# A mixture-of-experts stage on Trainium2: second products entered before the last activations, and an output finished in two parts

## What is computed

```python
probs = softmax(xt @ Wr + br)
top_p, top_idx = jax.lax.top_k(probs, 2)
weights = top_p / top_p.sum(-1)
xn = (xt - mu) * rsqrt(var + 1e-5)
xe = xn[None] * ln_g[:, None] + ln_b[:, None]
h = gelu(einsum('end,edh->enh', xe, W1) + b1)
y = einsum('enh,ehd->end', h, W2) + b2
out = x + sum over the node's two experts of weight * y
```

## Time and profile before

| what | us |
|---|---|
| median of 3 runs | 2840.2 |
| the profiled execution, its own time | 2840.06 |
| span of the profiled execution | 2838.0 |
| share of the span with PE busy | 83% |

### The profile page before, as it was taken

The page is one execution under the profiler, slowest core; times in us unless marked ns, Lnnn a source line. Parts: engine busy times, 40 slices in busy tenths (PEclk is TensorE's granted clock), DMA queues, the critical chain, the costliest instruction groups (busy, mean ns, idle before and its releaser), DMA issues.

```text
span 2838.0 us, 39531 instructions
## 1 busy us (share of the span) xinstructions
PE 2366.4 (83%) x14254; PEld 1777.4 (63%) x14254; DVE 1033.1 (36%) x2750; ACT 450.3 (16%) x1227; POOL 884.5 (31%) x661
## 2 busy tenths in 40 slices
PE   5185552577859999999997889999999995999997
PEld 2151110354547777777775457888888894888886
DVE  7688885233321111112115854112211455111111
ACT  0030000000015100003203742001111003222222
POOL 6888888887840000000003320000000001333332
PEclk6595555798979999999999999999999996999999
DMA  9922223886460899992144000444344434667665
GB/s 337 317 1 0 0 1 48 237 225 182 69 181 15 176 221 258 227 209 82 58 151 146 1 1 12 148 143 138 127 139 151 160 121 139 204 191 228 189 206 169
DMA packets 298688, 397.91 MB, mean 140 GB/s; under 512 B 178182, under 2 KB 242125, under 8 KB 298507
## 3 DMA queue, kind: packets, MB, share of 16 engines
q1 hardware_dynamic: 115530, 268.24, 29.7%
q10 hardware_dynamic: 110560, 108.20, 15.5%
q0 software_dynamic: 72496, 20.10, 8.4%
HBM read 279.36 MB, written 99.82 MB: 134 GB/s over the span
## 4 chain that ended last, share of the span: by engine, by line
PE 63%; POOL 20%; issue 7%; DVE 5%; DMA 3%; ACT 1%; DVEq 0%; SPq 0%; ACTq 0%; POOLq 0%
PE ps L2085 14%; POOL odd_counts L622 10%; POOL at_counts L622 10%; PE ps L2414 9%; PE ps L2416 9%; PE ps L2510 7%; PE ps L2501 7%; PE ps L2011 5%; PE ps L2103 3%; PE ps L2216 2%; PE ps L2370 2%; PE ps L2347 2%; DMA odd_counts<-harena 1%; PE ps L2262 1%; PE ps L2483 1%
## 5 line engine op out<-in xcount | busy, mean ns | idle before, releaser
L2414 PE MATMUL ps<-harena,ring 128*128 128x257 f16 (+1 forms) x2500 | 540.3, 272 | 5.2 <-DVE harena L1728 3.9
L2416 PE MATMUL ps<-harena,ring 128*128 128x256 f16 x2400 | 534.4, 271 | 0.0
L2085 PE MATMUL ps<-ring,harena 128*128 128x320 f16 (+1 forms) x3740 | 506.9, 298 | 1.4 <-ACT tarena L830 0.8
L2085 PEld LDWEIGHTS ps<-ring,harena 128*128 128x128 f16 x3740 | 367.1, 98 | 138.0 <-issue 3.1
L622 POOL DMA_INDIRECT at_counts<-harena x208 | 327.3, 1574 | 81.7 <-issue 79.0
L622 POOL DMA_INDIRECT odd_counts<-harena x208 | 328.9, 1581 | 67.1 <-issue 62.5
L1250 DVE SCALAR_TENSOR_TENSOR late<-ps,ring 128x512 f16<-128x512 f32 x416 | 287.4, 746 | 20.8 <-PE ps L1973 9.7
L1973 PE MATMUL ps<-harena,ident 104*128 104x512 f32 x208 | 186.1, 1011 | 116.7 <-DVE late L1250 115.7
L2414 PEld LDWEIGHTS ps<-harena,ring 128*128 128x128 f16 x2500 | 243.1, 97 | 40.3 <-DVE harena L1728 6.1
L2416 PEld LDWEIGHTS ps<-harena,ring 128*128 128x128 f16 x2400 | 232.2, 97 | 29.9
L700 POOL IOTA harena<- 1x32 int32 x1 | 0.2, 184 | 685.5 <-DVE xrows L1810 685.5
(11 more groups left out here) (418 smaller groups left out, 2459.1 us busy)
## 6 DMA issues: line engine op xcount, KB each, us to landing
ring<-at_counts SPq DMA_DIRECT2D x145, 800.0 KB
ring<-L_ffn_W SPq DMA_DIRECT2D x64, 1024.0 KB, 5.3
ring<-ad_counts SPq DMA_DIRECT2D x50, 800.0 KB
at_counts<-tarena ACTq DMA_DIRECT2D x5, 4000.0 KB, 21.5
odd_counts<-tarena ACTq DMA_DIRECT2D x5, 4000.0 KB
ad_counts<-xrows ACTq DMA_DIRECT2D x25, 800.0 KB, 7.7
xrows<-odd_counts SPq DMA_DIRECT2D x20, 800.0 KB
at_counts<-ring ACTq DMA_DIRECT2D x20, 800.0 KB
```

Of the source, the lines that this page charges most:

```text
L2085: ins = M(ps[:, 2 * f + h, 0:c], part[:, t, (2 * k + f) * P:(2 * k + f + 1) * P], chunk[q][:, s, h * HB:h * HB + c], start=(t == 0 and par ...
L2414: ins = M(ps[:, i, 0:wide], lhs, hh[:, t, 0:wide], start=(t == 0), stop=(t == T - 1))
L2416: ins = M(ps[:, i, 0:F], lhs, hl[:, t, :], start=False, stop=False)
```

## The change

There are four edits.

The diff:

```diff
--- before.py
+++ after.py
@@ -273,6 +273,8 @@
         xn = runs(tarena[:, T * F:2 * T * F], a=T)
         hot_lane = runs(tarena[:, 0:2 * T * P], a=2 * T)
         hot_column = harena[:, 0:2 * T * 2 * SC].rearrange("p (j v c) -> p j v c", j=2 * T, v=2)
+        final_row, same_row = hot_lane[:, 0, :], hot_lane[:, 1:1 + CT, :]
+        in_both = late[:, 2490:2490 + CT]
         w1e = [ring[:, s * 4096:s * 4096 + 2048].rearrange("p (d h) -> p d h", d=2) for s in range(2)]
         w2e = [ring[:, s * 4096 + 2048:(s + 1) * 4096].rearrange("p (k o) -> p k o", k=EK) for s in range(2)]
         hT = [harena[:, s * 2048:(s + 1) * 2048].rearrange("p (k n) -> p k n", k=EK) for s in range(2)]
@@ -573,11 +575,12 @@
                     sp.nop(nofuse=True)
                     load_second(e, s)
 
-            sp.wait_ge(y_used, CHUNKS + 2)
-            for b in range(0, NB, 2):
+            sp.wait_ge(y_used, CHUNKS)
+            for b in range(NB):
                 r = slice(b * BC, min((b + 1) * BC, N))
                 sp.dma_start(out[r, :], x_sum[r, :]).then_inc(out_stored, 16)
             sp.wait_ge(out_stored, 16 * NB)
+            sp.wait_ge(y_added, 16 * SC)
 
 
         @block.gpsimd
@@ -746,7 +749,7 @@
             gather_rows(2)
             pool.wait_ge(moe_stored, 16 * 5)
             pool.wait_ge(r_dve, 4)
-            for c in range(CHUNKS):
+            for c in range(CHUNKS - 2):
                 pool.wait_ge(e_y, c + 3)
                 for i in range(UNITS_OF[c]):
                     j = UNIT_AT[c] + i
@@ -757,6 +760,20 @@
                     gather_rows(c + 3)
                 pool.wait_ge(y_added, 16 * sum(UNITS_OF[:c + 1]))
                 pool.sem_inc(y_used, 1)
+
+            for c in (CHUNKS - 2, CHUNKS - 1):
+                pool.wait_ge(e_tps, c + 1)
+                for i in range(UNITS_OF[c]):
+                    j = UNIT_AT[c] + i
+                    nc.gpsimd.indirect_dma_start(out=xin[c % 2][:, i, :], out_offset=None, in_=x_sum,
+                                                 in_offset=bass.IndirectOffsetOnAxis(ap=from_row[:, j:j + 1], axis=0)).then_inc(row_in[c % 2], 16)
+            pool.wait_ge(out_stored, 16 * NB)
+            for c, rows, done in ((CHUNKS - 2, xin[0], CHUNKS + 2), (CHUNKS - 1, yrow[1], CHUNKS + 3)):
+                pool.wait_ge(e_y, done)
+                for i in range(UNITS_OF[c]):
+                    j = UNIT_AT[c] + i
+                    nc.gpsimd.indirect_dma_start(out=out, out_offset=bass.IndirectOffsetOnAxis(ap=to_row[:, j:j + 1], axis=0),
+                                                 in_=rows[:, i, :], in_offset=None, bounds_check=N - 1, oob_is_err=False).then_inc(y_added, 16)
 
 
         @block.scalar
@@ -1086,10 +1103,6 @@
                     for k in range(EK):
                         wait(e_hps, g * (TURN * EK) + (j * EK + k + 1))
                         nc.scalar.activation(hT[s][:, k, 0:n], ps[:, k % 4, 0:n], ACT.Gelu, bias=evc[s][:, k:k + 1]).then_inc(e_gelu, 1)
-            wait(y_used, CHUNKS + 2)
-            for b in range(1, NB, 2):
-                r = slice(b * BC, min((b + 1) * BC, N))
-                act.dma_start(out[r, :], x_sum[r, :]).then_inc(out_stored, 16)
 
 
         @block.vector
@@ -1916,6 +1929,14 @@
             step(V.tensor_tensor(slot_pad, slot_pad, trash_row[:, :], ALU.mult))
             step(V.tensor_tensor(slot_pad, slot_pad, slot_node, ALU.add))
             V.tensor_scalar(to_row, slot_pad, -1.0, None, ALU.add).then_inc(r_dve, 1)
+            V.tensor_scalar(final_row, ident[:, :], slot_pad[:, SC - 1:SC], None, ALU.mult).then_inc(r_dve, 1)
+            dve.wait_ge(r_pe, 4)
+            last_pair = slice(UNIT_AT[CHUNKS - 2], UNIT_AT[CHUNKS - 2] + CT)
+            o.mark(V.tensor_tensor(same_row, ps[:, 7, 0:P].unsqueeze(1).to_broadcast([P, CT, P]), slot_pad[:, last_pair].unsqueeze(2).to_broadcast([P, CT, P]), ALU.is_equal))
+            o.settle()
+            step(V.tensor_reduce(in_both, same_row, AX.X, ALU.max))
+            step(V.scalar_tensor_tensor(out=in_both, in0=in_both, scalar=float(2 * T * P), in1=slot_pad[:, last_pair], op0=ALU.mult, op1=ALU.add))
+            o.mark(V.tensor_scalar(to_row[:, last_pair], in_both, -1.0, None, ALU.add))
 
             def expert_rows(c, uses, s, n):
 
@@ -1933,13 +1954,34 @@
                 step(V.tensor_tensor(rows, ps[:, 4 + s, 0:k * F].rearrange("p (i c) -> p i c", i=k), b2e[s].unsqueeze(1).to_broadcast([P, k, F]), ALU.add))
                 V.tensor_tensor(rows, rows, slot_gate[:, bass.ds(unit, k)].unsqueeze(2).to_broadcast([P, k, F]), ALU.mult).then_inc(e_y, 1)
 
+            def pair_finished():
+
+                dve.wait_ge(row_in[0], 16 * (sum(UNITS_OF[0::2]) + CT))
+                dve.wait_ge(e_y, CHUNKS + 1)
+                V.tensor_tensor(xin[0], xin[0], yrow[0], ALU.add).then_inc(e_y, 1)
+
+            def single_finished():
+
+                gate = slot_gate[:, SC - 1:SC]
+                dve.wait_ge(row_in[1], 16 * (sum(UNITS_OF[1::2]) + 1))
+                dve.wait_ge(w2e_in[1], 32 * (CHUNKS // 2))
+                dve.wait_ge(e_yps, CHUNKS + 2)
+                step(V.tensor_tensor(xin[1][:, 0, :], xin[1][:, 0, :], ps[:, 6, 0:F], ALU.add))
+                step(V.scalar_tensor_tensor(out=xin[1][:, 0, :], in0=b2e[1], scalar=gate, in1=xin[1][:, 0, :], op0=ALU.mult, op1=ALU.add))
+                dve.wait_ge(e_yps, CHUNKS + 3)
+                dve.wait_ge(y_used, CHUNKS)
+                V.scalar_tensor_tensor(out=yrow[1][:, 0, :], in0=ps[:, 5, 0:F], scalar=gate, in1=xin[1][:, 0, :], op0=ALU.mult, op1=ALU.add).then_inc(e_y, 1)
+
             def turn_of_chunks(g, last):
 
                 for j in range(TURN):
                     c, s = g * TURN + j, j % 2
-                    if not (last and j == TURN - 1):
+                    if last and j == TURN - 1:
+                        pair_finished()
+                        single_finished()
+                    else:
                         expert_rows(c + 1, g * (TURN * 8) + ((j + 1) // 2 * 16 + 16), 1 - s, UNITS_OF[(j + 1) % TURN] * P)
-                    chunk_out(c, s, g * (CT * (TURN - 1)) + CT * j if j < TURN - 1 else g + CT * PAIRS, UNITS_OF[j])
+                        chunk_out(c, s, g * (CT * (TURN - 1)) + CT * j if j < TURN - 1 else g + CT * PAIRS, UNITS_OF[j])
 
             expert_rows(0, 16, 0, CAP)
             with o.loop(SINGLES - 1, TURN) as g:
@@ -2503,10 +2545,12 @@
 
             def outputs(gelu, y, wi, s, n):
                 pe.wait_ge(w2e_in[s], wi)
-                pe.wait_ge(e_gelu, gelu)
+                pe.wait_ge(e_gelu, gelu - 2)
                 pe.wait_ge(e_y, y)
                 for i in range(n):
                     for k in range(EK):
+                        if i == 0 and k >= EK - 2:
+                            pe.wait_ge(e_gelu, gelu - EK + 1 + k)
                         ins = M(ps[:, 4 + s, i * F:(i + 1) * F], hT[s][:, k, i * P:(i + 1) * P], w2e[s][:, k, :], start=(k == 0), stop=(k == EK - 1))
                 ins.then_inc(e_yps, 1)
 
@@ -2521,10 +2565,17 @@
                     final = last and j == TURN - 1
                     if not final:
                         turn_rows(rows_of(g, j + 1), 1 - s, m)
+                    else:
+                        pe.wait_ge(e_y, CHUNKS + 1)
+                        for i in range(CT):
+                            ins = M(ps[:, 6, 0:F], same_row[:, i, :], yrow[0][:, i, :], start=(i == 0), stop=(i == CT - 1))
+                        ins.then_inc(e_yps, 1)
                     outputs(g * (TURN * EK) + (j * EK + EK + 1), g * TURN + (j + 1), g * (TURN * 16) + (j // 2 * 32 + 32), s, n)
                     if not final:
                         hidden(g * (TURN * 2) + (2 * j + 4), g * (TURN * EK) + (j * EK + EK + 1), g * (TURN * 8) + ((j + 1) // 2 * 16 + 16), 1 - s, m)
 
+            pe.wait_ge(r_dve, 5)
+            M(ps[:, 7, 0:P], ones[:, :], final_row, start=True, stop=True).then_inc(r_pe, 1)
             turn_rows(16 * CT, 0, CT)
             hidden(2, 1, 16, 0, CT)
             with pe.Fori(0, SINGLES - 1) as g:
```

## The result

The changed kernel takes 2812.4 us, the median of 6 runs (2811.5 to 2823.6), beside 2841.4 for the kernel before in the same group of runs. The ratio is 0.9904, 95% interval 0.9886 to 0.9922. In a later group of runs it was 2812.3 (6 runs), ratio 0.9898 (0.9882 to 0.9914). The ratios in this document are estimates over a group's runs and not quotients of its medians. Forecast were 2821.5 and a range down to 2816.5, so the change gives 28 us (by the two profiles) where 18.7 were forecast.

A forecast was written before the change was run, and what follows sets the result against it. PE was taken to bound the experts' stage, followed by a serial end of 17.8 us with PE idle. Gaps (8.5) and the end (10.2) take 18.7 us off the 2840.2 median: 2821.5, range 2816.5 to 2828.

The forecast's parts named there:

- the gaps: PE's waits ahead of the second products: 9.7 us over 32 chunks, all taken as gained, 8.5 of the forecast saving.
- Rival 3: Gaps ahead of second products don't close fully, or inner waits cost 0.06 each: +3.8 us, 2825.3; 12%.
- That six of eight is enough: Entering second products: the sixth activation ends early enough never to bind; seventh and eighth, needed 2.7 us in, are long done.
- Inner waits at nothing: Waits added inside the second products: priced at nothing; 0.12 us for each of 64 would give back 7.7.
- Ahead of the first chunk: Five DVE operations and one matmul added there are hidden, except that the first may hold the first gather: +0.2 us.
- rival 4: Granted clock ahead of chunk 0's first products: the added matmul could move its rise either way, up to 3.2 us; 10%.
- The tail from chunk 29's second scatter: From chunk 29's scatters landed to the end: 29.9 us now, 19.7 in the change, with two chunks beside the copies.
- the copies: All five on SP's queue at the end: 12.7 us from issue, starting at 2799.6 and landed at 2812.3.
- Plain scatters: Three on POOL at the end: 1.0 us each with 0.3 between, first at 2813.4, POOL done at 2817.0.
- The gathers: Partial sums fetched by POOL beside the copies: held up by the copies' packets, landing at about 2812.2.
- rival 1: Gathers at the end not held up by the copies' packets: POOL goes on at 2812.6, 0.8 us earlier, 2820.7; 10%.
- Rival 2: Copies at the end run slower on one queue or beside the gathers: up to +4 us, 2825.5; 13%.

The follow-up runs named there:

- edit 1 alone: Kernel before, with only the second products entered on six of eight activations and waits for the last two inside; 2822.6 us, ratio 0.9918.
- e6: The change with seven waits instead of two inside the first unit's second products; 2813.8 us.
- e2: The change with the second products' wait for all eight activations put back; 2829.9 us, ratio 0.9926 to the kernel before.
- e5: The change with second products entered on seven of eight activations, one inner wait instead of two; 2814.3 us.
- e7: The change without the three gathers of partial sums, so part of the output is left out; 2819.6 us in one run.
- the change again: The changed kernel, unaltered, measured once more in a later group; 2812.3 us, ratio 0.9898 to the kernel before.

## Why the prediction was wrong

The profile gives 28.0 us where 18.7 were forecast. Of the 9.3 more, 7.7 are the gaps, the step that failed, and 1.5 are chunk 0's clock, which was luck. With chunk 0 as before it would be 26.4 and the time near 2814, still below the range.

- **The gaps: the step that failed.** The working says "so 9.7 us in all" of the waits in the earlier trace rows, and later "I take all 9.7 us as gained": the wait shown was taken for what the wait costs. It costs 17.9 us, in the run with edit 1 alone and in the change. Of the 8.2 beyond 9.7, 32 x 0.16 = 5.1 are the passing-through that an idle row doesn't count, and 32 x 0.09 = 2.9 the first weight load, which the wait holds too; 0.2 stay unassigned. The first was in the profile of before: 7.07 shown in the timeline and 6.91 in the chain for the same matmuls. Rival 3 looked only for gaps that close less than fully.
- **That six of eight is enough** held, with the margin forecast: not one wait is left. With seven of eight no wait is shown either, but the held weight load costs 0.08 in seven chunks.
- **Inner waits at nothing** held: 64 in the change, and 160 more in e6 for nothing.
- **Ahead of the first chunk.** The +0.2 was for a first gather that the first added DVE operation holds. It isn't held: it starts while that operation runs, and 0.86 us after its table is written (L1927 ends at 2395.28), as before (2390.31 to 2391.17).

```profile
2395.09 0.19 DVE L1927 TENSOR_SCALAR harena<-harena 128x56 int32<-128x56 f32 x1
...
2396.02 0.28 DVE L1932 TENSOR_SCALAR tarena<-ident,harena 128x128 f32<-128x128 f32 x1
2396.14 1.15 POOL L741 DMA_INDIRECT harena<-xn_rows,harena  x1 [18.00 <-DVE harena L1931]
```

The same four DVE operations lie between table and gather in both kernels, the last of them (L1931) ending 0.04 ahead of the gather, so whether they hold it stays open. By the port rule of the Trainium skill (SBUF — State Buffer, "Who interferes with whom") the gather would have waited for L1932 if that runs in a two-port mode; this trace shows no such wait. The rule's other case, two SBUF inputs, counts only against a GpSimd instruction that reads SBUF, which the forecast left out. The +0.14 of the first piece lies behind the gather's start and has no cause shown.
- **Chunk 0's clock** (rival 4) gave 1.5 us in this profile and 1.5 in the change again, but nothing in e2, e5 and e7 (10.12, 10.16 and 10.04), which have the same added matmul. It varies without the change, and can't be credited to it.
- **The tail from chunk 29's second scatter** came out as forecast, 26.5 us for 26.5, because two errors cancel; that is luck too. The scatter landed after 5.13 where 6.8 to the copies' issue were taken (5.2 measured, 1.6 less); the copies took 14.2 to land where 12.7 were taken to the end of their data and semaphores (1.5 more; without the gathers beside them it was 12.0). Plain scatters took about 1.0 each, the first 1.19; POOL was done 5.0 after the copies had landed (forecast 4.7), and the end followed 2.1 later (2.3).
- **The gathers** landed 8 to 10 us after their issue, near the copies' end, as forecast. The pair's addition began 12.4 us after the first copy's issue (12.8 forecast). But it was done 1.1 us before the copies had landed, and POOL was released by the copies, which is what rival 1 said of POOL. Rival 2 came true in part: the copies were 1.5 us slower, where it allowed up to 4.

## What to carry to other kernels

What a stop of PE costs is read from starts: the time from one group's start to the next, less the same group's time where nothing waits. The idle shown here was 0.30 us a chunk and the cost 0.56. When an accumulation waits for its last inputs, let it begin on the ones that are there; here the inner waits, once met, cost nothing to be seen, and the weight loads got back under the work ahead. When a tail is moved beside other work, count what else ends there: here the next bound after copies, gathers and scatters was POOL's own end.

## What was not expected of the hardware

- A stop on PE costs 0.25 us beyond its shown idle time: 0.16 of overlap and 0.09 of an uncovered fp32 weight load (478 ns for 379). The second part is also paid where only the load is held and no idle time shows (463 ns in e5).
- The end of POOL's program comes 6.1 us after its last indirect DMA or its last wait with 112 indirect DMAs in this stage, and 1.8 to 1.9 us after the last one with 115.
- An indirect DMA of 128 rows costs POOL about 1.0 us as gather or plain scatter, with the bounds check too (0.94 to 1.19 in the rows seen), and 1.58 when it accumulates.
